# The last up job of a shared expert moved behind the expert slots, and the first slot's rows turned one job earlier

## The reference

```python
x = x + jnp.tanh(g_xattn[0]) * _L0_xattn_ref(_layernorm(x), ctx_4096, Wq, Wk, Wv, Wo)
x = x + jnp.tanh(g_ffn[0]) * _L0_ffn_ref(_layernorm(x), ...)
# in _L0_ffn_ref, with xt of 2048 x 512:
...
    h = jax.nn.silu(xt @ w1 + b1) * (xt @ w2 + b2)          # one expert, 512 -> 128
    return (y + ge[:, None] * (h @ w3 + b3), None)          # 128 -> 512, weighed by its gate
y, _ = jax.lax.scan(step, jnp.zeros_like(xt), (ew1, eb1, ew2, eb2, ew3, eb3, gate.T))
z = jax.nn.silu(xt @ sw1 + sb1) * (xt @ sw2 + sb2) @ sw3 + sb3   # shared expert, 512 -> 256 -> 512
return (y + z).reshape(shape)
```

## Time and profile before

| | |
|---|---|
| runs | median 1545.6 us of 3 (1543.26 to 1545.85) |
| the profiled execution | 1544.32 us, its span 1542.6 us |
| busy, share of the span | PE 95%, PE weight loads 85%, DVE 63%, ACT 50%, POOL 12% |
| mean granted TensorE clock | 0.987 of full |

### The profile page before, as it was taken

The page is one execution under the profiler, slowest core; times in us unless marked ns, Lnnn a source line. Parts: engine busy times, 40 slices in busy tenths (PEclk is TensorE's granted clock), DMA queues, the critical chain, the costliest instruction groups (busy, mean ns, idle before and its releaser), DMA issues.

```text
span 1542.6 us, 26300 instructions
## 1 busy us (share of the span) xinstructions
PE 1470.0 (95%) x9136; PEld 1306.0 (85%) x9136; DVE 973.8 (63%) x1632; ACT 779.0 (50%) x2028; POOL 188.0 (12%) x198
## 2 busy tenths in 40 slices
PE   7999988999999999999999999999999999888986
PEld 5888878999999999989999989999998778887874
DVE  5322237666677666666766657776666778666657
ACT  3112216555566555555655546555555545676760
POOL 0000000000000000000000000000003423677750
PEclk9999999999999999999999999999999999999998
DMA  7576542111223111132211122221110303677528
GB/s 233 162 228 168 138 163 96 48 63 54 68 76 109 64 42 48 66 107 69 74 50 69 41 70 76 82 90 42 48 49 15 110 29 110 226 239 251 162 83 327
DMA packets 97447, 163.67 MB, mean 106 GB/s; under 512 B 12435, under 2 KB 47287, under 8 KB 93258
## 3 DMA queue, kind: packets, MB, share of 16 engines
q1 hardware_dynamic: 87370, 145.62, 29.0%
q0 software_dynamic: 9984, 16.82, 3.3%
HBM read 128.29 MB, written 49.81 MB: 115 GB/s over the span
## 4 chain that ended last, share of the span: by engine, by line
PE 69%; issue 6%; DVE 4%; ACT 2%; SPq 2%; DMA 1%; another core or an unknown queue 1%; ACTq 0%; DVEq 0%
PE ps_q L84 8%; PE ps_q L86 8%; PE ps_q L85 8%; PE ps_y L85 8%; PE ps_y L84 8%; PE ps_y L86 8%; PE ps_s L1008 5%; PE ps_p L1048 4%; PE ps_o L84 2%; PE ps_s L1010 2%; PE ps_o L86 2%; PE ps_o L85 2%; PE bank L84 1%; PE bank L86 1%; PE bank L85 1%
## 5 line engine op out<-in xcount | busy, mean ns | idle before, releaser
L84 PE MATMUL ps_q<-xt,wq_hi 128*128 128x256 f32 x1024 | 302.6, 295 | 4.4 <-PEq L118 4.4
L86 PE MATMUL ps_q<-xt,wq_hi 128*128 128x256 f32 x1024 | 291.7, 285 | 0.0
L85 PE MATMUL ps_q<-xt,wq_lo 128*128 128x256 f32 x1024 | 291.7, 285 | 0.0
L842 ACT ACTIVATE s_sb<-s_sb,nmax 128x128 f32<-128x128 f32 x512 | 199.9, 392 | 129.7 <-DVE nmax L924 129.7
L922 DVE TENSOR_TENSOR s_sb<-ps_s,s_cross 128x512 f32<-128x512 f32 x128 | 88.4, 691 | 232.4 <-ACT s_cross L831 232.2
L831 ACT ACTIVATE s_cross<-ps_s 128x512 f32<-128x512 f32 x128 | 76.5, 597 | 272.3 <-PE ps_s L1010 272.3
L84 PE MATMUL ps_y<-wo_hi,o_hi 128*128 128x512 f32 x512 | 202.3, 395 | 0.9 <-DVE y L902 0.9
L86 PE MATMUL ps_y<-wo_lo,o_hi 128*128 128x512 f32 x512 | 202.6, 396 | 0.0
L85 PE MATMUL ps_y<-wo_hi,o_lo 128*128 128x512 f32 x512 | 202.6, 396 | 0.0
L84 PEld LDWEIGHTS ps_q<-xt,wq_hi 128*128 128x128 f32 x1024 | 196.9, 192 | 5.0 <-issue 4.8
L85 PEld LDWEIGHTS ps_q<-xt,wq_lo 128*128 128x128 f32 x1024 | 197.1, 193 | 0.0
(11 more groups left out here) (262 smaller groups left out, 3230.3 us busy)
## 6 DMA issues: line engine op xcount, KB each, us to landing
xt<-x_scratch SPq DMA_DIRECT2D x32, 1024.0 KB, 4.9
w_raw<-in_L_ffn_ew SPq DMA_DIRECT2D x93, 256.0 KB
v_full<-v_out SPq DMA_DIRECT2D x64, 128.0 KB, 2.6
k_full<-k_out SPq DMA_DIRECT2D x16, 512.0 KB, 2.8
w_raw<-in_L_xattn_Wq SPq DMA_DIRECT2D x16, 512.0 KB, 5.1
kt_raw<-k_full SPq DMA_DIRECT2D x32, 256.0 KB, 2.6
vt_raw<-v_full SPq DMA_DIRECT2D x32, 256.0 KB, 2.7
w_raw<-in_L_xattn_Wo SPq DMA_DIRECT2D x16, 512.0 KB, 4.3
```

Source lines behind the costliest of these rows:

```text
L84: pe.matmul(out, w_hi, x_hi, start=first, stop=False)
L85: pe.matmul(out, w_lo, x_hi, start=False, stop=False)
L86: return pe.matmul(out, w_hi, x_lo, start=False, stop=last)
L842: last = act.activation(s_sb[:, i], s_sb[:, i], ACT.Exp, bias=nmax[:, i:i + 1], accum_out=sums[:, i:i + 1])
```

## The change

Job 7 leaves its place before the slots and stands behind them. Its 24 matmuls on PE, its two ACT evacuations and its copy, and its product and low part on DVE follow the last slot on each engine, and on PE they stand ahead of all `pe_down`. What changes with it:

- `turn(0)` moves between the two parts of job 6.
- Job 6 takes half 1 and job 7 half 0 of the last octet (`part`), and the memory is laid out anew so that the half 0 weights live through the slots (`y2_late` takes their place later, and the last two loads of SP wait for job 7).
- On ACT and DVE the high and low part of job 6 move into slot 0, and ACT waits there for `sh_lo` of jobs 0 to 6 before the slot's silu.
- Job 7 uses banks 0 and 1; the order of the banks of `pe_down` and the places of its waits change.

```diff
+    def part(self, j):
+        o = j // 2
+        return o, 1 - j % 2 if o == OCTETS - 1 else j % 2
...
     def pair(self, j):
-        return self.ps_up[2 if j == self.JOBS - 1 else j % 2]
+        return self.ps_up[j % 2]
...
     def act_high(self, act, j):
         act.wait_ge(self.h_made, j + 1)
-        act.wait_ge(self.up_done, j // 2 * 2 + 2)
+        if j != self.JOBS - 2:
+            act.wait_ge(self.up_done, j // 2 * 2 + 2)
...
-        y2_pairs += [buf[:, 0:2] for buf in (*rows_in, *w_raw)]
+        y2_pairs += [buf[:, 0:2] for buf in (*rows_in, w_raw[0])] + y2_late
...
             for q in range(TILES // 2):
+                if q == TILES // 2 - 1:
+                    sp.wait_ge(shared.up_done, shared.JOBS)
                 for i in range(2):
                     sp.dma_start(y2[q][i], choices_v[q, i]).then_inc(y2_in[q], 16)
... # ACT, in slot()
+                if isinstance(s, int) and s == 0:
+                    shared.act_high(act, LATE - 1)
+                    act.wait_ge(shared.h_lo_made, LATE)
                 act.wait_ge(up_done, s + 1)
... # ACT, around the slots
             xs_high(0, 0)
-            shared.act_up(act, 7)
-            shared.act_high(act, 6)
-            shared.act_high(act, 7)
-            act.wait_ge(shared.h_lo_made, shared.JOBS)
             over_slots(act, slot)
             evacuate(LAST, LAST % 2)
+            shared.act_up(act, LATE)
+            shared.act_high(act, LATE)
... # DVE, in slot()
+                if isinstance(s, int) and s == 0:
+                    shared.dve_low(dve, LATE - 1)
... # DVE, around the slots
-            shared.dve_product(dve, 7)
-            shared.dve_low(dve, 6)
-            shared.dve_low(dve, 7)
             over_slots(dve, slot)
+            shared.dve_product(dve, LATE)
+            shared.dve_low(dve, LATE)
... # PE
-            for part in range(2):
-                shared.pe_up(pe, 6, part)
+            shared.pe_up(pe, 6, 0)
...
             pe.wait_ge(shared.gate_copied, 6)
             turn(0, 0)
-            for part in range(2):
-                shared.pe_up(pe, 7, part)
+            shared.pe_up(pe, 6, 1)
             pe.wait_ge(slots_made, 3)
             over_slots(pe, slot)
             down(LAST, LAST % 2)
+            for part in range(2):
+                shared.pe_up(pe, LATE, part)
             pe.wait_ge(small_lo_made, 4)
             pe.wait_ge(gates_lo_made, OCTETS)
-            pe.wait_ge(shared.h_lo_made, shared.JOBS)
             for n in range(TILES):
-                if n in (3, 6):
-                    pe.wait_ge(y_out_made, 2 * SLOTS - 2 if n == 3 else 2 * SLOTS)
+                if n in (1, 4):
+                    pe.wait_ge(y_out_made, 2 * SLOTS - 2 if n == 1 else 2 * SLOTS)
+                if n == 6:
+                    pe.wait_ge(shared.gate_copied, shared.JOBS)
+                if n == TILES - 4:
+                    pe.wait_ge(shared.h_lo_made, shared.JOBS)
                 shared.pe_down(pe, n)
```

More of the change, by code:

```diff
@@ L1147, in pair @@
     def pair(self, j):
-        return self.ps_up[2 if j == self.JOBS - 1 else j % 2]
+        return self.ps_up[j % 2]
     def act_up(self, act, j):
-        r, half = j % self.DEEP, j % 2
+        r, half = j % self.DEEP, self.part(j)[1]
         act.wait_ge(self.up_done, j + 1)
@@ L1164, in act_high @@
         act.wait_ge(self.h_made, j + 1)
-        act.wait_ge(self.up_done, j // 2 * 2 + 2)
-        act.activation(self.h[j // 2][j % 2][0][:], self.h_sb[j % self.DEEP][:], ACT.Copy).then_inc(self.h_hi_made, 1)
+        if j != self.JOBS - 2:
+            act.wait_ge(self.up_done, j // 2 * 2 + 2)
+        o, half = self.part(j)
+        act.activation(self.h[o][half][0][:], self.h_sb[j % self.DEEP][:], ACT.Copy).then_inc(self.h_hi_made, 1)
     def dve_product(self, dve, j):
@@ L1175, in dve_low @@
     def dve_low(self, dve, j):
-        h_hi, h_lo = self.h[j // 2][j % 2]
+        o, half = self.part(j)
+        h_hi, h_lo = self.h[o][half]
         dve.wait_ge(self.h_hi_made, j + 1)
@@ L1185, in pe_up @@
     def pe_up(self, pe, j, k, lo=0, hi=C):
-        o, half = j // 2, j % 2
+        o, half = self.part(j)
         if k == 0 and lo == 0:
@@ L1189, in pe_up @@
                 pe.wait_ge(self.w_lo_made, half + 1)
-            elif j == self.JOBS - 1:
-                pe.wait_ge(self.gates_copied, OCTETS)
             else:
@@ L1233, in stage_three @@
             for o in range(OCTETS):
-                h.append([[e.sb(f"sh_{part}{half}{o}", [P, 512], F32R) for part in ("hi", "lo")] for half in range(2)])
+                if o < OCTETS - 1:
+                    h.append([[e.sb(f"sh_{part}{half}{o}", [P, 512], F32R) for part in ("hi", "lo")]
+                              for half in range(2)])
+                else:
+                    h.append([[e.sb(f"sh_{part}0{o}", [P, 512], F32R) for part in ("hi", "lo")], beside])
                 if o == 0:
@@ L1238, in stage_three @@
                     b3 = e.sb("b3", [3 * 32, D], F32R)
-                    e.sb("apart5", [P, 3 * 512])
+                    beside = [e.sb(f"sh_{part}1{OCTETS - 1}", [P, 512], F32R) for part in ("hi", "lo")]
+                    e.sb("apart5", [P, 512])
                 if o == 2:
@@ L1269, in stage_three @@
             hot_col = [e.sb("hot_col0", [P, TILES // 2, 2, COLS])]
-        y2_early = [b.sb(f"y2_early{i}", [P, 2, D])[:] for i in range(3)]
+        y_out = [b.sb(f"y_out{i}", [P, 2, D]) for i in range(2)]
+        y2_early = [b.sb("y2_early0", [P, 2, D])[:]]
         with ExitStack() as up_front:
@@ L1273, in stage_three @@
             sw_up = [[e.sb(f"sw_up_{part}0", [P, 2, 512], F32R) for part in ("hi", "lo")]]
-        y_out = [b.sb(f"y_out{i}", [P, 2, D]) for i in range(2)]
+        y2_late = [b.sb(f"y2_late{i}", [P, 2, D])[:] for i in range(2)]
         sw_down = [[b.sb(f"sw_down_{part}0", [P, 512], F32R) for part in ("hi", "lo")]]
@@ L1386, in stage_three @@
         shared = SharedExpert(b, sw_up, sw_down, x_hi, x_lo, s_silu, s_h_sb, h,
-                              [banks[4:6], banks[0:2], banks[6:8]], [banks[i] for i in (0, 1, 3, 6, 7, 2, 4, 5)], y,
+                              [banks[4:6], banks[0:2]], [banks[i] for i in (3, 6, 7, 2, 4, 5, 0, 1)], y,
                               common["shared_bias"], bias_copied, gates_copied, stacked, b3)
@@ L1451, in stage_three @@
         LAST = SLOTS - 1
+        LATE = SharedExpert.JOBS - 1
         def late(s, m):
```

## The result

| | before | after |
|---|---|---|
| median, us (13 runs each) | 1545.85 | 1550.21 |
| ratio, with its 95% interval | | 1.0035 [1.0024, 1.0047] |
| profiled execution, us (span) | 1544.3 (1542.6) | 1547.9 (1546.2) |

The change costs about 5.4 us by the ratio (0.0035 x 1546; its interval is 3.7 to 7.3, and the medians differ by 4.4). The direction was forecast, at half the size (1548.3, which is +2.7 on the median of the three runs; the sum itself was +3.2). Two profiled executions differ ahead of the change too, by a few us, so I count from a matmul that both kernels have just before it: the last one that puts `bias_rows_lo` into the slots' biases. Call it B; it starts at 1293.61 before and at 1290.21 after.

A forecast was written before the change was run, and what follows sets the result against it. It took the end as bound by the last slot, eight down products on PE, DVE's 24.5 us of additions and one store; +5.6 - 2.3 - 0.1 = +3.2 us gave 1547.5 profiled, 1548.3 stated, range 1545.5 to 1551.

The forecast's parts named there:

- the sum: Whole kernel: +5.6 at the end, -2.3 at the start, -0.1 for the last store, together +3.2 us.
- Job 7 bare at the end: Behind the last slot, ahead of the down products: nothing covers job 7's 24 matmuls on PE, so +5.6 us.
- The transfers don't set the end: Tail: DVE's 24.5 us of additions set the end, with transfers some 5 us ahead; the opposite rival had chance 0.09.
- Two idle pieces ahead of the turns, 1.6 and 3: Before slot 0: PE waits 1.6 us for gathered rows ahead of `turn(0)` and about 3.1 us ahead of `turn(1)`.
- I take 1298.3: Before slot 0: the assumed landing of the gathered rows that `turn(0)` needs, between 1296.7 and 1299.4.
- "-2.3" at the start: Slot 0: `h_sb(0)` comes at 1310.5 instead of 1312.78, a gain of 2.3 us (bounds -3.2 and -1.2).
- the chain at full clock: Slot 0: the steps from `xs_high(0)` to `h_sb(0)`, forecast at 6.6 us.
- Clock drop: Rival, chance 0.22: idle PE ahead of up(0) halves its clock, losing 0.7 to 2.4 us of gain; sum +3.9 to +5.6.
- It is ACT and DVE that are relieved, not PE.: Start of the slots: the 2.3 us gain comes from ACT and DVE no longer doing job 7's part first.
- If slot 0 moves by some amount, I expect the ring to move by that amount and no more.: Slot loop: ACT, DVE and two weight buffers form a ring of dependent rounds, which shifts exactly as slot 0 does.
- the second rival: No shift, chance 0.12: transfers pace the slots' ring or it takes the start back; gain 0 to 1, sum +4.6 to +5.6.
- its sign of being wrong: Slots: the forecast is wrong in kind if the slot stage is not 194 us long from `h_sb(0)` on.

The follow-up runs named there:

- e3: Changed kernel with job 7 cut to 6 of its 24 matmuls (its result incomplete); 1549.36 us, ratio 1.0014 to the kernel before.
- v_tail: Changed kernel with job 7 between PE's eighth and ninth down product, its DVE product and subtraction between the additions; 1548.47 us, ratio 1.0013 to before.
- e1: Changed kernel with 12 more matmuls behind part 1 of job 6, filling PE's idle piece ahead of `turn(1)`; 1551.79 us, ratio 1.0031 to before.
- e4: Changed kernel without the second addition of the first four pairs of token tiles on DVE (result incomplete); 1553.28 us, ratio 1.0038 to before.
- u_after: Changed kernel with its 31 slots written out instead of looped; 1550.97 us, ratio 1.0031 to before.
- u_before: Kernel before with its 31 slots written out instead of looped; 1543.05 us, ratio 0.9981 to before.
- e6: Changed kernel's new buffers, but with job 7 back ahead of the slots as in the kernel before; 1547.17 us, ratio 0.9999 to before.
- light_before: Kernel before with the weight loads of slots 2 to 30 cut to 8 of 128 partitions; 1546.28 us, ratio 1.0015 to before.
- d_late: Kernel before with job 7's gate half computed three times ahead of the slots (24 matmuls more); 1552.14 us, ratio 1.0051 to before.
- short_in_place: Kernel before with 18 of job 7's 24 matmuls left out at its old place (result incomplete); 1532.83 us against 1535.23, ratio 0.9976.
- u_both: Changed kernel with slots written out, `xs_high(0)` ahead of `act_up(6)`, and job 7 behind the eighth down product; 1542.99 us, ratio 0.9983 to before.
- e2: Changed kernel with `xs_high(0)` ahead of `act_up(6)` on ACT and `xs_low(0)` ahead of `dve_low(5)` on DVE; 1552.15 us, ratio 1.0034 to before.
- xs_short: Changed kernel with e2's order and e3's short job 7 (result incomplete); 1535.38 us against 1535.23 for the kernel before, ratio 1.0002.
- s_both: Changed kernel with e2's order, half of job 6's second part ahead of `turn(0)`, and job 7 behind the eighth down product; 1533.99 us, ratio 0.9992 to before.
- s_xs: Changed kernel with e2's order and half of job 6's second part ahead of `turn(0)`; 1536.90 us against 1534.47 for the kernel before, ratio 1.0010.
- light_xs_first: Changed kernel with e2's order and the weight loads of slots 2 to 30 cut to 8 of 128 partitions; 1549.66 us, ratio 1.0030 to before.
- u_xs_short: Changed kernel with e2's order, e3's short job 7 (result incomplete) and its 31 slots written out; ratio 1.0001 to before.
- us_both: The kernel of s_both with its 31 slots written out; 1535.56 us, ratio 1.0007 to before.

## Why the prediction was wrong in size

- *Job 7 bare at the end, +5.6.* Right: +5.5 in the profile; e3 takes 18 matmuls away and gets 18 x 0.23 back; v_tail gives DVE something to do meanwhile and pays 1.8.
- *The transfers don't set the end.* Right; DMA share 0.57 in the last 12 us.
- *Two idle pieces ahead of the turns, 1.6 and 3.* Right in the profile (1.78, 3.29). But the first is not one number: over the 11 profiles with `turn(0)` in the middle of job 6 it is 1.33 to 3.01, since the rows land 4.6 to 6.2 us after B. "I take 1298.3", 4.7 after B, was near the early end. Before, `turn(0)` at 5.81 hid nearly all of it.
- *"-2.3" at the start.* **This is the step that failed.** In the profile it is +0.2, and with it the sum becomes +5.7, against +5.4 timed. Of the 2.5 us missing, 0.4 is in `xs_high(0)`, 0.3 of it the later rows; 1.8 is the half clock in `turn(1)` and up(0) (8.7 us from `xs_high(0)` against 6.9 in e1 and e3); 0.3 is the chain at full clock (6.9 against 6.6). The clock is thus the largest part and not the whole: e3, which keeps it at 1.00, starts 1.4 us early and not 2.3. Over six profiles of that order at `turn(0)` and ACT (after, e1, e3, e4, v_tail, u_after) the start is +0.2, -0.4, -1.4, -1.2, -1.1, +1.1, mean -0.4.
- *Clock drop as a rival with 0.22.* The chance was too low. Nine of 14 profiles with the new place of `turn(0)` show the half clock at one of the two places or both; of the six profiles that keep the old one (before, u_before, e6, light_before, d_late, short_in_place) none does. With the mean start the sum is +5.1, within the rival's +3.9 to +5.6, and its 1549.5 is nearer to 1550.2 than the forecast. The Trainium skill ("TensorE: Matmul & The Clock Gate", section on HAM oscillation) says of a matmul kernel with waits of some 3 to 5 us between its bursts that the clock comes down at each of them. These runs agree in most executions, not in all: of the six idle pieces of 3.29 us or more ahead of `turn(1)`, five have the half clock behind them and that of e3 has not, and in u_both the half clock stands behind a piece of 1.90 us.
- *"It is ACT and DVE that are relieved, not PE."* Half wrong, as short_in_place shows: PE's 4.2 us alone are worth 2.5 there.
- *"If slot 0 moves by some amount, I expect the ring to move by that amount and no more."* Right within what times can tell. d_late pays its 5.5, short_in_place gains its 2.5, light loads change nothing. With the mean starts of each order (-0.4, -2.0, -2.8) instead of a single profile's, e2 should be at +3.5 (timed 3.4 to 7.0), e3 at +1.0 (0.3 to 4.0), xs_short at -0.7 (-1.7 to 2.3), s_both at -1.0 (-2.9 to 0.5). e4 (+3.3, timed 3.7 to 8.0) lies outside, and short_in_place (-1.9, timed -5.4 to -2.0) by a tenth. What stays open: e2, e3, e4 and xs_short were timed 1.0 to 2.6 us above their sums, s_xs and s_both 0.2 to 1.2 below theirs, and whether more than chance is in that can't be said. The profiles leave room for a part of the second rival: in five pairs from one result or one chip (after and before, u_after and u_before, v_tail and e6, light_xs_first and light_before, xs_short and short_in_place) the stretch from `h_sb(0)` to `h_lo(30)` is longer by 1.3, 1.3, 0.5, -0.5 and 1.0 us in the changed order. Four kernels of one chip (e1 to e4) lie between 189.7 and 191.6, so single profiles can't tell such a difference from chance.
- *Slips of the sum that change nothing.* By the prediction's own terms `turn(1)` starts 0.88 ahead of up(0), at 1305.6, and PE is idle from 1302.2, which is 3.4 us and not 3.1 (measured 3.29). And its sign of being wrong, a slot stage that is not 194 us from `h_sb(0)` on, takes the wrong stretch: 194.2 us go from the first up(0), and from `h_sb(0)` to `h_lo(30)` it is 186.2 in the kernel before already.

That the total of +5.4 is so near to the tail's +5.5 is then no law: the clock and the rows' landing eat the start in this order of work, on average nearly all of it.

## What to carry to other kernels

A job moved behind a loop costs its full length if the next engine's unbroken run starts behind it; ask first which engine has work in hand there (DVE had, eight additions later). A gain at the start of a stage that is bought with idle pieces of TensorE must be counted with what they may do to its clock, and with the latest landing of the transfer that it waits for, not with the landing in one profile. And a length that one execution shows (a landing, a slot stage) is one draw: align two profiles at a common instruction, and take the spread from several kernels that share the place.

## What the runs showed that I had not expected

**The clock after equal waits.** 3.29 us of idleness ahead of the same eight transposes: granted clock 0.50 behind it in one execution, 1.00 in another. With it a matmul of 256 columns in up(0) takes 0.41 or 0.28 us.

**ScalarE's stops in the loop of slots.** Slots follow each other every 5.8 to 5.9 us, but in the loop every second one takes 6.6 or 7.3. Waits of ACT in 1312 to 1490 (total us, times, longest), for before, for u_before and for light_before:

```profile
ACT silu L1728 <- remote: 16.1, 12, 2.3
```

```profile
ACT silu L1723 <- remote: 11.3, 6, 3.0
```

```profile
ACT silu L1729 <- remote: 21.6, 10, 4.4
```

A stop ahead of the silu that the profile can put down to nothing on the core comes once per turn of the two-slot loop; written out, it comes every third slot, in all 5 us less, and the kernel is 3 us faster. That the one makes the other is argued, not shown: the slots as a whole are only 0.8 us shorter in the profile of u_before. Less transfer traffic does not shorten it. On the two chips that timed xs_short, u_xs_short, short_in_place, s_xs, s_both and us_both it is absent; the waits of ACT in short_in_place, 1312 to 1480, are all that there are:

```profile
ACT h_hi L1733 <- DVE h_sb L1925: 40.2, 28, 1.5
ACT w_hi L1702 <- DMA w_raw<-in_L_ffn_ew: 4.7, 7, 1.8
```

There the 31 slots take 178 to 180 us instead of 183 to 192, the kernel before has medians of 1535.2 and 1534.5 instead of 1544.7 to 1547.7, and writing out the slots gains nothing. My guess in u_before was that ScalarE waits for code behind the loop's jump. The kept traces speak against it, as far as their queues show transfers of code. From 1340 to 1475, where before has 11 of these stops and short_in_place none, both move the same two packets of that kind, and u_before, with fewer stops, moves 14. The line of before (queue, packets, MB, share):

```profile
q14 instruction: 2, 0.02, 0.0%
```

What the stops are, and why chips differ, stays open.
